# Expert stage of a graph layer: the scatter's wait for the scatter before it moves to tiles that open a new expert

## The reference

```python
logits = xf @ router_w
gate_vals, idx = jax.lax.top_k(logits, K)        # K = 2
gates = jax.nn.softmax(gate_vals, axis=-1)
...
for e in range(E):                               # E = 8
    h = jax.nn.relu(xf @ w1[e] + b1[e]) @ w2[e] + b2[e]
    y = _layernorm(xf + h, gamma[e], beta[e])
    w = jnp.sum(jnp.where(idx == e, gates, 0.0), axis=-1)
    out = out + w[:, None] * y
...
x = x + ffn(_layernorm(x))
```

## Time and profile before

| | |
|---|---|
| median of 3 runs | 3566.81 us (3551.92 to 3568.43) |
| the profiled execution | 3556.41 us, its span 3554.6 us |
| granted TensorE clock, mean | 0.947 |
| TensorE busy | 2883.6 us (81%) |
| VectorE busy | 2069.3 us (58%) |
| GpSimd busy | 1745.2 us (49%) |
| ScalarE busy | 1468.0 us (41%) |
| moved by DMA | 131 GB/s over the span |

### The profile page before, as it was taken

One profiled execution on the slowest core, in us unless ns is written; L12 is line 12 of the kernel. 1 busy time (PEld: TensorE's weight loads), 2 busy tenths in 40 slices (PEclk: granted clock), 3 DMA queues, 4 the chain that ended last, 5 costly groups with the idle time before them and its releaser, 6 DMA issues. The chain is left out here.

```text
span 3554.6 us, 70114 instructions
## 1 busy us (share of the span) xinstructions
PE 2883.6 (81%) x13011; PEld 1583.4 (45%) x13012; DVE 2069.3 (58%) x5410; ACT 1468.0 (41%) x3850; POOL 1745.2 (49%) x1847
## 2 busy tenths in 40 slices
PE   4989899999974777778878888888888658877884
PEld 4945566666652222222333333333333335555553
DVE  4567798877765344545455555555555555555554
ACT  2545511111112444444454545555555334444442
POOL 1255511122322666666556565656656365555554
PEclk9999999999997989999999999999999769999997
DMA  4245400111112556556656566666666635555553
GB/s 162 85 138 164 143 26 28 37 41 47 53 53 72 168 161 173 174 172 181 181 175 192 177 189 185 195 181 196 195 194 195 210 104 90 89 90 90 89 90 59
DMA packets 203167, 465.85 MB, mean 131 GB/s; under 512 B 43732, under 2 KB 56391, under 8 KB 201962
## 3 DMA queue, kind: packets, MB, share of 16 engines
q0 software_dynamic: 100448, 318.23, 33.9%
q1 hardware_dynamic: 102669, 147.07, 13.1%
HBM read 385.15 MB, written 79.93 MB: 131 GB/s over the span
## 5 line engine op out<-in xcount | busy, mean ns | idle before, releaser
L1053 PE MATMUL acc_ps<-rows,W 128*128 128x512 f32 x1908 | 1047.5, 657 | 327.7 <-DMA rows<-h_rows,idx 170.1
L940 POOL DMA_INDIRECT rows<-h_rows,idx x954 | 966.4, 1013 | 702.8 <-issue 288.9
L1053 PEld LDWEIGHTS acc_ps<-rows,W 128*128 128x128 f32 x1908 | 320.5, 199 | 997.4 <-issue 778.3
L978 ACT ACTIVATE e_pos<-pqb,es_col 128x128 f32<-128x128 f32 x954 | 373.2, 391 | 241.2 <-issue 202.3
L1150 DVE TENSOR_TENSOR e_top<-e_pos,e_neg 128x384 f32<-128x384 f32 x318 | 173.6, 556 | 369.9 <-ACT e_neg L979 204.1
L979 ACT ACTIVATE e_neg<-pqb,es_col 128x128 f32<-128x128 f32 x954 | 368.5, 386 | 21.3 <-issue 21.2
L1156 DVE SCALAR_TENSOR_TENSOR W<-window,dst_col,e_top 128x128 f32<-128x128 f32 x954 | 278.7, 347 | 165.8 <-issue 101.7
L1568 PE MATMUL hid_ps<-xsT,w_now 128*128 128x128 f32 x1680 | 220.7, 287 | 109.6 <-issue 96.4
L700 DVE TENSOR_SCALAR masked<-p_window,dst_col,hi_col 128x128 f32<-128x128 f32 x954 | 281.7, 366 | 43.7 <-DVE p_window L692 41.4
L973 ACT COPY idx<-src_col 128x2 int32 x477 | 80.3, 186 | 546.7 <-SPq L922 280.1
L1534 POOL DMA_INDIRECT out<-y,idx_add x105 | 172.8, 1646 | 228.2 <-DMA out<-y,idx_add 165.2
(11 more groups left out here) (260 smaller groups left out, 4329.0 us busy)
## 6 DMA issues: line engine op xcount, KB each, us to landing
lo_row<-src_lo SPq DMA_DIRECT2D x102, 256.0 KB, 3.3
rows<-h_rows,idx POOLq DMA_INDIRECT x954
xb<-in_x SPq DMA_DIRECT2D x49, 256.0 KB, 2.7
h_rows<-hb SPq DMA_DIRECT2D x49, 256.0 KB, 2.1
fold_w<-in_x SPq DMA_DIRECT2D x49, 256.0 KB, 2.6
res_rows<-fold_w SPq DMA_DIRECT2D x49, 256.0 KB, 2.0
a_own<-h_rows SPq DMA_DIRECT2D x49, 256.0 KB
a_xr<-res_rows SPq DMA_DIRECT2D x49, 256.0 KB
```

The lines of the kernel that those rows point to most:

```text
L940: nc.gpsimd.indirect_dma_start(G[j][:], None, h_rows, bass.IndirectOffsetOnAxis(ap=idx[:, j:j + 1], axis=0)).then_inc(row_in[j], 16)
L978: nc.scalar.activation(e_pos[:, half, j, :], pqb[s][:, 0, :], ACT.Exp, bias=es_col[:, ds(at_tile + (half * HT + j), 1)])
L1053: nc.tensor.matmul(acc_ps[s][:], W[:, j, :], G[j][:], start=(opens and j == 0), stop=(j == VT - 1), skip_group_check=True).then_inc(row_us ...
```

## The change

- `nobody` has 128 columns in place of one: the spare row of an empty slot is NP + p in tiles of even number and NP + 128 + p in tiles of odd number. `xf_rows` and `out` are 128 rows longer, and SP writes zeros to both sets of spare rows.
- Behind the packing of the experts DVE works out, for each tile, a bit that is 1 where its expert is a later one than that of the tile before, and packs eight tiles a word into `opens_pack`.
- POOL loads two words of `opens_pack` into registers every eight turns (`with_openings`), and takes from them the bit of the tile whose scatter comes.
- From tile 4 on, the scatter of tile t waits for the scatter of t-1 where the bit is 1. Where it is 0 it waits for one scatter of that semaphore fewer, that of t-3. Tiles 1 to 3 wait as before. The wait of DVE for the scatter of t-2, before it writes `y`, stays.

```diff
-        "nobody": NP + np.arange(P)[:, None] + 1,
+        "nobody": NP + np.arange(P)[:, None] + 1 + P * (np.arange(P)[None, :] % 2),
...
-    xf_rows = dram("xf_rows", [NP + P, D + NE])
+    xf_rows = dram("xf_rows", [NP + 2 * P, D + NE])
...
-                        sp.dma_start(xf_rows[NP:NP + P, :], nobody[:]).then_inc(kept, 16)
-                        sp.dma_start(out[NP:NP + P, :], nobody[:, 0:D]).then_inc(kept, 16)
+                        for b in (NP, NP + P):
+                            sp.dma_start(xf_rows[b:b + P, :], nobody[:]).then_inc(kept, 16)
+                            sp.dma_start(out[b:b + P, :], nobody[:, 0:D]).then_inc(kept, 16)
...
                         step(V.tensor_copy(expert_pack[:], packed[:]))
+                        step(V.tensor_copy(opens[:], owner[:]))
+                        step(V.tensor_tensor(opens[:].rearrange("o g k -> o (g k)")[:, 1:], flat[:, 1:], flat[:, 0:packs * PK - 1], ALU.is_gt))
+                        step(V.tensor_copy(opens_f[:], opens[:, :, 0]))
+                        for k in range(1, PK):
+                            step(V.scalar_tensor_tensor(opens_f[:], opens[:, :, k], float(2 ** k), opens_f[:], ALU.mult, ALU.add))
+                        step(V.tensor_copy(opens_pack[:], opens_f[:]))
                         dve.wait_ge(hot_used, NT // QT)
-                        step(V.tensor_scalar(unlisted[:, 0:ST], token_ps[:, 0:ST], 0.0, C["nobody"], ALU.is_equal, ALU.mult))
+                        step(V.scalar_tensor_tensor(unlisted[:, 0:ST], token_ps[:, 0:ST], 0.0, C["nobody"][:, 0:ST], ALU.is_equal, ALU.mult))
...
+                def with_openings(eng, steps):
+
+                    found = None
+                    for n, lags in enumerate(steps):
+                        k = next(k for k, one in enumerate(lags) if one)
+                        tau = lags[k][0] + k
+                        if n % PK == 0:
+                            j = tau // PK if isinstance(tau, int) else lags[k][2] + (lags[k][1] + k) // PK
+                            if not isinstance(j, int) or j > 0:
+                                _, found = nc.values_load_multi_w_load_instructions(opens_pack[:, ds(j - 1, 2)], [eng.engine], min_val=0, max_val=2 ** PK - 1)
+
+                        def opens_expert(back, at=n % PK + 4 + PK, both=found):
+                            return (both[(at - back) // PK] >> (at - back) % PK) & 1
+
+                        yield opens_expert, lags
...
-                                if not isinstance(t, int) or t > 0:
+                                if not isinstance(t, int) or t >= 4:
+                                    hold(pool, y_out[1 - s], (opens_expert(10) + (i2 + s - 1)) * 16)
+                                elif t > 0:
                                     hold(pool, y_out[1 - s], 16 * i2 + 16 * s)
```

More of the change, by code:

```diff
@@ L1250, in gps_layer @@
             expert_pack = sb(ex, "expert_pack", [1, packs], I32)
+            opens_pack = sb(ex, "opens_pack", [1, packs], I32)
             weights_in = sem("expert_weights_in")
@@ L1266, in gps_layer @@
                 at_or_past, owner, packed = sb(ro, "at_or_past", [1, packs * PK, NE]), sb(ro, "owner", [1, packs, PK]), sb(ro, "packed", [1, packs])
+                opens, opens_f = sb(ro, "opens", [1, packs, PK]), sb(ro, "opens_f", [1, packs])
                 QT = 7
@@ L1294, in _ @@
                             sp.dma_start(b2_split[k, :].rearrange("(p c) -> p c", p=P), b2_piece[k][:]).then_inc(kept, 16)
-                        sp.wait_ge(kept, 96)
+                        sp.wait_ge(kept, 128)
                         sp.dma_start(b2_part[:].rearrange("k e d -> k (e d)"), b2_split).then_inc(kept, 16)
-                        sp.wait_ge(kept, 112)
+                        sp.wait_ge(kept, 144)
                     @block.gpsimd
@@ L1516, in _ @@
                         pool.wait_ge(weights_in, 16 * 5)
-                        for now, _, _, _, _, _, _, _, back8, _, back10 in lagged(pool, ST, 10, 1, R8):
+                        for opens_expert, (now, _, _, _, _, _, _, _, back8, _, back10) in with_openings(pool, lagged(pool, ST, 10, 1, R8)):
                             if back8:
@@ L1695 @@
     a = {n[3:]: nc.dram_tensor(n, v.shape, mybir.dt.from_np(v.dtype), kind="ExternalInput").ap() for n, v in arrays.items()}
-    out = nc.dram_tensor("out", (NP + P, D), F32, kind="ExternalOutput").ap()
+    out = nc.dram_tensor("out", (NP + 2 * P, D), F32, kind="ExternalOutput").ap()
     gps_layer(nc, a, out)
```

## The result

The changed kernel takes **3449.61 us** in the median of 4 runs (3446.08 to 3458.41), the kernel before on the same chip 3565.47 us (3551.92 to 3568.43, 4 runs). The ratio is 0.9686, its 95% interval [0.9655, 0.9717]. The forecast was 3420 us within 3400 to 3478: inside the range, 30 us above the likeliest value. The profiled execution took 3448.29 us, its span is 3446.5.

The account below looks back on a forecast made before the run. Bound: the wait for each scatter's landing, 5.895 us a tile, no engine full. Terms: -145.1 beat, +5 openings, +1.7 routing, +0.25 constants, -3 tail, sum -141 us, giving 3420 us, range 3400 to 3478.

Parts of the forecast that it names:

- forecast case: Whole kernel: the chosen outcome, 3420 us, with ends at 3402 and 3443 us; chance 66%.
- 4.5 us a tile: Scatter stage: beat expected without the landing wait, in place of 5.895 us, a gain of 145.1 us over 104 beats.
- POOL's pace: POOL's queue per tile in the scatter stage: 4.43 us, between 4.19 and 4.55, with a scatter of 1.62 us.
- TensorE's 4.45 us: TensorE in the scatter stage: its own pace per tile, from bias products of four tiles in a row without idle shown.
- The two buffers y: Loop through VectorE's y and the scatter of t-2: 8.13 us for two tiles, 4.07 a tile, so not the bound.
- Openings: At most seven tiles that open an expert still wait, 1.35 us each; between 0 and 9.4 us, 5 taken.
- Routing: Eleven added DVE steps, 2.9 us, less 1.20 us of idle cover: 1.7 us more on the path.
- Tail: End of the stage: last scatters follow each other faster than at 4.5 us, about 3 us less, between 0 and 6.
- 1, the queue: POOL's queue sets the pace, with a 0.58 us gap at every scatter: 5.0 us a tile, 3474 us; chance 14%.
- 2, the lock: VectorE and GpSimd share locked SBUF ports, so each POOL scatter takes 2.13 us: 4.94 a tile, 3468 us; chance 5%.
- 3 and 4, longer landings: Scatter landings grow when scatters follow closer: at 6.5 us, 3456 us (chance 9%); at 9 us, 3588 us (chance 3%).
- 5: Opening bits come out as 1 everywhere, every scatter waits as now: 3568 to 3579 us; chance 3%.

Follow-up runs that it names:

- e3: Changed kernel with every opening bit written as 1, so each scatter waits as in the kernel before: 3331.54 us, ratio 1.0003 to the kernel before.
- e6: Changed kernel with the two zn buffers in PSUM in place of SBUF, timed beside the unaltered changed kernel: 3206.54 us, ratio 0.9616 to the kernel before.
- e5: Changed kernel run again unaltered, as base of its group: 3226.08 us, ratio 0.9665 to the kernel before.
- e1: Changed kernel with the two zn buffers in PSUM in place of SBUF, first run: 3203.54 us, ratio 0.9622 to the kernel before.
- e2: Kernel before, with only the two zn buffers moved from SBUF to PSUM: 3323.73 us, ratio 0.9971 to the kernel before.
- e4: Changed kernel with every tile taking expert 0, without expert-number loads and shifts on three queues: 3209.44 us, ratio 0.9635 to the kernel before.
- e9: Changed kernel with zn in PSUM and every tile taking expert 0, without expert-number loads: 3387.01 us, ratio 0.9608 to the kernel before.
- e8: Changed kernel with 128 own output rows per tile, and without opening bits, their load and register instructions on POOL: 3216.88 us, ratio 0.9646 to the kernel before.
- e7: Changed kernel with each scatter adding into 128 own rows and all opening bits zero, loads and registers kept: 3220.92 us, ratio 0.9652 to the kernel before.

## Why the prediction came out as it did

**The mechanism was right.** Landings left the path and the pace of the engines took over; e3 shows that nothing else in the change gives anything, or costs anything under the old beat. But the measured 3449.61 us lie above the upper end of the forecast case, 3443. They are in the range only because it was drawn wide enough for rivals 2 and 3 and most of 1.

**The step that was mis-sized is the 4.5 us a tile**, with -145.1 us for it. The stage became 113.4 us shorter, where the sum had 145.1 - 5 + 3 = 143.1 with openings and tail. The missing 30 us are two terms:

- POOL's pace was summed with a scatter of 1.62 us. It is 1.855 with VectorE's multiply at its start: 18 us by e6 against e5. The rule of the skill was read and given 5% as a rival, at 2.13 us for each scatter; the truth was half of that extra, in nearly every ordinary tile. The 0.08 us between 1.54 and 1.62 that the prediction took for all that the rows show of the rule is not its doing at all: 1.62 is what a scatter takes with the lock out of the way (e1), and 1.54 that of the last two. What the rows did hold was the 22 longer scatters, up to the 2.13 of the earlier trace rows, and set beside what VectorE ran at their start (e2 above) they give the price of a meeting exactly. What they could not show is how often the meeting would happen, and with which operation: behind a landing the multiply was over and only `y` was there, and not always.
- TensorE's 4.45 us came from four tiles in a row that no load on ScalarE or VectorE reached. Those loads, one round in eight tiles on three engines, cost 12.7 us of the stage with the lock (e5 - e4) and 14 without (e6 - e9). The sum priced the new load on POOL, at 0.14 us a tile, and forgot the old ones. Yet the next row held their cost: the 0.80 us of idle time ahead of `hid_ps` at 2944.79 was read as the first that TensorE felt of the landings. It stands at the same place, 13.7 us behind the first scatter, in the changed kernel (0.78) and in e6 (0.75), and is missing in e4 and e9, which have no loads: it is that of ScalarE's load, at 2941.3. The landings begin to tell one tile later. The new load, on POOL, runs while the scatter executes.

Taken off the stage of e5, the two make 498.3 - 18.0 - 12.7 = 467.6 us; e9 has 466.4. The forecast's own stage is 613.1 - 143.1 = 470.0, so what it describes is nearly the kernel without these two. That it fits so well is in part luck, for two more errors cancel. **Tiles 1 to 3** wait as before, and the sum gave them the 1.4 us of gain like all others: their beats are 5.92, 5.83 and 5.79 us in the changed kernel, 4.0 us in all over three of 4.5. Against that, the pace between openings in e9 is 4.40 in place of 4.5. That two level paces make something slower than each was an argument of mine that e9 doesn't bear out: with POOL at 4.39, TensorE ran at 4.40.

**POOL's register instructions**: 0.1 us was taken for the two. The gap is 0.2 us longer, and e8 gives 0.28 for all three and what came with them; the price of it is 2 to 4 us in the whole at most, since the lock absorbs it.

**The two buffers y** (4.07 us a tile, not the bound): right. A landing released VectorE's `y` in 49 tiles, with 24.6 us of idle time in all, 0.50 us each, and 0.34 to 0.42 stands ahead of `y` where no landing does.

**Openings**: +5, measured 4.8 (e7). The number is right by luck, for the reason was another: what saves is not that TensorE ran ahead but that three of the seven fell beside a round of loads; the other four cost 0.8 to 1.2 us each of the 1.35 that the sum had.

**Routing**: +1.7. These rows answer to the earlier trace rows:

```profile
2895.88 0.21 DVE L1454 COPY opens<-owner 1x120 f32<-1x120 f32 x1
2896.12 0.27 DVE L1455 TENSOR_TENSOR opens<-owner 1x119 f32<-1x119 f32 x1
2896.43 0.16 DVE L1456 COPY opens_f<-opens 1x15 f32<-1x15 f32 x1
2896.63 1.37 DVE L1458 SCALAR_TENSOR_TENSOR opens_f<-opens,opens_f 1x15 f32<-1x15 f32 x7
2898.03 0.16 DVE L1459 CAST opens_pack<-opens_f 1x15 int32<-1x15 f32 x1
2898.22 0.27 DVE L1461 SCALAR_TENSOR_TENSOR unlisted<-token_ps,cst 128x105 f32<-128x105 f32 x1
```

The steps take 2898.22 - 2895.88 = 2.34 us, not 2.9 (the strided copy is 0.16, not 0.75), and less the cover of 1.20 that makes 1.1. The first scatter is 4.8 us later in this trace, but the stages ahead of it move by as much between executions of the same or nearly the same code (its start is at 2713.3 in e5, 2719.5 in e7), so the rest is not put down to the change.

**SP's zeros and the constants**: nothing can be seen of them, as forecast; e3 holds them too.

**Tail**: -3. The last nine beats of the changed kernel take 37.6 us, 2.9 less than nine of 4.5, though one or two of them hold a round of loads; it was not tried apart.

**Rivals.** 1, the queue: its gap is real, 0.58 us in each tile as it said, but its 5.0 us a tile counted 0.38 of that twice and did not see that the lock takes such a gap back. 2, the lock: the right mechanism, at two fifths of the price (18 us of stage, forecast as 0.44 x 104 = 46 more than the chosen case). 3 and 4, longer landings: at openings the scatters of e6 are 5.4 to 5.9 us apart, less 0.94 a landing of 4.4 to 5.0, as in the earlier trace rows. In the changed kernel they are 5.9 to 6.3 apart, which makes 5.0 to 5.4 with a scatter that the lock lengthens. Between openings the traces give no landing; even 5.4 everywhere would leave the loop through `y` at (5.4 + 3.22) / 2 = 4.3 us a tile, an estimate by the prediction's own formula, while the changed kernel's ordinary tiles take 4.6. 5: excluded, and e3 shows that it would have cost less than I said.

## What to carry to other kernels

When a wait is removed, the prices of what stood beside it are not the medians of its trace: list the operations that used to start after the wait, ask which of the other engine's operations they will now meet, and look among the longest instances of each for what a meeting costs. Take an engine's pace from a period that holds everything which comes round (here eight tiles, with their register loads), not from the cleanest tiles, and ask of an idle time marked "issue" what stands in the queues before it is put down to the wait under study. And where two engines exclude each other, time taken out of one's queue ahead of the meeting point is given back in the meeting; move an operand instead.

## Seen of the hardware

- A scatter issued by POOL ended 1.49 us behind the end of a VectorE operation with two SBUF operands that ran at its start: the multiply (81 scatters of the changed kernel, 1.47 to 1.51) or `y` (22 of the kernel before, 1.49 to 1.51). It took 1.62 us where there was none, where one operand was in PSUM, or where at most 0.13 us of the operation was left. The operation itself kept its 0.69 or 0.75 us. One that started after the scatter had begun did not lengthen it and was not lengthened: `y`, 0.8 us into it in ordinary tiles, and in e5 a multiply 0.11 us into it (0.68 us, the scatter 1.62).
- A register load of two words took 0.49 us on ScalarE, 0.53 to 1.23 on TensorE and 0.52 to 1.18 on VectorE. In the kernel before the long ones were TensorE's, in the changed kernel mostly VectorE's. In a stage without slack one round of them costs about 1 us in all.
- An operation's place in the queue can be free while it looks dear: POOL's own new load took 0.53 us, fourteen times, and no beat shows it.
